# Vision-transformer tower: the last tile's root, normalizing and transposes moved inside four layernorms, fewer products of zeros, and row scatters placed behind a copy

## The reference, cut to what matters

```
h = patches @ W + positions                                  # 592 x 256
h = h + attention(_layernorm(h))                             # 16 heads, rotary parts      (layernorm 0)
h = h + moe_8_experts_top_2(_layernorm(h))                   # shared expert + 8 routed    (layernorm 1)
h = h + selective_scan(_layernorm(h))                        # 16 states, 37 steps         (layernorm 2)
h = h + moe_64_experts_top_8(_layernorm(h))                  # shared expert + 64 routed   (layernorm 3)

def _layernorm(x, axis=-1, eps=1e-05):
    m = jnp.mean(x, axis=axis, keepdims=True)
    v = jnp.var(x, axis=axis, keepdims=True)
    return (x - m) / jnp.sqrt(v + eps)
```

## Time and profile before

| | us |
|---|---|
| median of three executions | 437.95 |
| the profiled execution, its own time | 443.19 |
| its span from first to last instruction | 441.5 |
| PE busy | 415.7 |
| DVE busy | 255.6 |
| ACT busy | 139.9 |
| POOL busy | 156.1 |

### The profile page before, as it was taken

The page is one execution under the profiler, slowest core; times in us unless marked ns, Lnnn a source line. Parts: engine busy times, 40 slices in busy tenths (PEclk is TensorE's granted clock), DMA queues, the critical chain, the costliest instruction groups (busy, mean ns, idle before and its releaser), DMA issues. The chain is left out here.

```text
span 441.5 us, 8821 instructions
## 1 busy us (share of the span) xinstructions
PE 415.7 (94%) x2977; PEld 333.0 (75%) x2985; DVE 255.6 (58%) x643; ACT 139.9 (32%) x352; POOL 156.1 (35%) x129
## 2 busy tenths in 40 slices
PE   8999999888997999999999899998998999999993
PEld 5665567766786999999976389886776788888872
DVE  0548878765850111221353789998775656655545
ACT  1040068783321111112204865552401223232210
POOL 2007834540056100010470168761001156545560
PEclk9999999999898999999999989999899999999998
DMA  8863096001067768874250233321025477787453
GB/s 265 234 174 114 2 293 234 3 1 57 1 254 263 254 211 255 282 265 141 88 163 35 80 110 109 106 62 43 15 72 152 150 180 198 174 201 176 109 128 105
DMA packets 32078, 63.57 MB, mean 144 GB/s; under 512 B 6063, under 2 KB 19678, under 8 KB 29742
## 3 DMA queue, kind: packets, MB, share of 16 engines
q1 hardware_dynamic: 26381, 50.90, 36.9%
q0 software_dynamic: 5664, 12.25, 10.9%
HBM read 50.51 MB, written 12.63 MB: 143 GB/s over the span
## 5 line engine op out<-in xcount | busy, mean ns | idle before, releaser
L1891 PE MATMUL PS<-xT,w1s 128*128 128x296 f32 x224 | 62.2, 422 | 0.0
L1891 PEld LDWEIGHTS PS<-xT,w1s 128*128 128x128 f32 x224 | 42.4, 195 | 11.7 <-issue 1.1
L1839 PE MATMUL PS<-ident,scratch 128*128 128x128 f32 (+1 forms) x340 | 43.6, 281 | 1.2 <-DVE scratch L1278 1.1
L629 POOL DMA_INDIRECT scratch<-xg,idx_nxt x18 | 17.9, 996 | 73.0 <-DVE idx_nxt L1412 38.6
L1272 DVE TENSOR_TENSOR_SCAN scratch<-scratch,PS 128x592 f32<-128x592 f32 x32 | 41.9, 1366 | 2.9 <-PE PS L1846 2.9
L1839 PEld LDWEIGHTS PS<-ident,scratch 128*128 128x128 f32 (+1 forms) x340 | 38.8, 183 | 5.2 <-DVE scratch L1278 2.2
L1195 DVE COPY scratch<-PS 128x144 f32<-128x144 f32 (+1 forms) x16 | 5.1, 319 | 64.2 <-PE PS L1765 64.2
L1756 PE MATMUL PS<-scratch,w0up 128*128 128x144 f32 (+1 forms) x256 | 37.6, 307 | 3.6 <-DVE scratch L1178 3.3
L1756 PEld LDWEIGHTS PS<-scratch,w0up 128*128 128x128 f32 x256 | 35.9, 196 | 5.6 <-DVE scratch L1178 4.2
L1906 PE MATMUL PS<-w1s,scratch 128*128 128x256 f32 (+1 forms) x140 | 34.7, 381 | 1.3 <-DVE h L1315 1.1
L785 ACT ACTIVATE scratch<-PS 128x288 f32<-128x288 f32 (+1 forms) x32 | 13.8, 430 | 67.8 <-PE PS L1756 59.6
(11 more groups left out here) (332 smaller groups left out, 756.9 us busy)
## 6 DMA issues: line engine op xcount, KB each, us to landing
w0dn<-in_w0dn SPq DMA_DIRECT2D x9, 1024.0 KB, 5.2
w0up<-in_w0up SPq DMA_DIRECT2D x9, 1024.0 KB, 5.9
w0dn<-in_w SPq DMA_DIRECT2D x16, 384.0 KB, 3.9
scratch<-rows_c SPq DMA_DIRECT2D x14, 296.0 KB, 3.3
by_expert<-zeros SPq DMA_DIRECT2D x2, 1920.0 KB, 13.2
w1s<-in_w SPq DMA_DIRECT2D x14, 256.0 KB
w1s<-in_w SPq DMA_DIRECT2D x14, 128.0 KB, 3.5
w0up<-in_patchesT SPq DMA_DIRECT2D x6, 296.0 KB, 4.6
```

The lines of the kernel that those rows point to most:

```text
L629: nc.gpsimd.indirect_dma_start(xe1[:, half, q, :], None, xg, bass.IndirectOffsetOnAxis(ap=idx_nxt[:, q:q + 1], axis=0)).then_inc(xe1_in[q] ...
L1839: last = mm(PS[0:ROWS[t], t // 2, (t % 2) * D + c * P:(t % 2) * D + (c + 1) * P], src[:, t * P:t * P + ROWS[t]], ident[:, :], start=False, ...
L1891: last = mm(PS[:, 2 * n + j, 0:HALF], w1s[:, s, w:w + F1], xT[:, c, half(n)], start=c == 0, stop=c == 1)
```

## The change

There are eight edits.

1. On POOL, the wait for `xeT_ready` moves from between the fourth and fifth scatter to ahead of the first.
2. On ACT, in every layernorm, the root of tile 4 moves ahead of the copy of the transposed tiles (L678).
3. On DVE, in layernorm 1 alone, the inverse and normalizing of tile 4 move ahead of the copy L914.
4. On DVE, in layernorm 2, `add_late(4)` moves from ahead of the inverse L901 to behind the normalizing of tiles 0 and 1.
5. On PE, for layernorms 0 and 3, the transposes of tile 4 move ahead of the products of tile 2.
6. On PE, for layernorm 1, ten products of zeros become five, three become one, and the transposes of tile 4 follow at once with two products of zeros behind them; they stood behind the logits of tiles 0 to 3.
7. On PE, four groups of four products of zeros ahead of layernorm 2's transposes become four groups of one.
8. On PE, behind layernorm 2, the transposes of tile 4 move between the two dt products of the first half, and the first quarter of u is made with the rest of u and no longer ahead of the second half of dt.

```diff
--- before.py
+++ after.py
@@ -556,9 +556,8 @@
                         bass.IndirectOffsetOnAxis(ap=idx0[:, s, j:j + 1], axis=0)).then_inc(xe_in[s], 16)
             for s in range(SLOTS0):
                 pool.wait_ge(y_out[s], 16)
+            pool.wait_ge(xeT_ready, 1)
             for t in range(NTILE):
-                if t == 2:
-                    pool.wait_ge(xeT_ready, 1)
                 for k in range(K0):
                     nc.gpsimd.indirect_dma_start(
                         rows_by_expert, bass.IndirectOffsetOnAxis(ap=slots[0:ROWS[t], k, t:t + 1], axis=0),
@@ -674,11 +673,10 @@
                 for t in (2, 3):
                     nc.scalar.activation(xn[:, t, :], normed_from(l, t), ACT.Identity, bias=xshift[:, t:t + 1],
                                          scale=rstd[:, t:t + 1]).then_inc(xn_act, 1)
+                act.wait_ge(var_ready, 2 * l + 2)
+                nc.scalar.activation(std[:, b:NTILE], mv[:, b:NTILE, 1], ACT.Sqrt, bias=LN_EPS).then_inc(std_ready, 1)
                 act.wait_ge(xT_mm, 2 * l + 1)
                 nc.scalar.copy(xT[:, 1, a * P:b * P], PS[:, XT_BANK[l] + 1, 0:(b - a) * P]).then_inc(xT_hi, 1)
-                a, b = LN_PARTS[1]
-                act.wait_ge(var_ready, 2 * l + 2)
-                nc.scalar.activation(std[:, a:b], mv[:, a:b, 1], ACT.Sqrt, bias=LN_EPS).then_inc(std_ready, 1)
 
             layernorm(0)
             for t in range(NTILE):
@@ -910,11 +908,17 @@
                 last_tile()
                 settle()
                 nc.vector.bn_aggr(mv[:, NTILE - 1, :], stats[:, NTILE - 1, :]).then_inc(var_ready, 1)
+                def normalize_last():
+                    dve.wait_ge(std_ready, 2 * l + 2)
+                    link(nc.vector.reciprocal(rstd[:, b:NTILE], std[:, b:NTILE]))
+                    normalize(NTILE - 1)
+
+                if l == 1:
+                    normalize_last()
                 dve.wait_ge(xT_mm, 2 * l + 1)
                 nc.vector.tensor_copy(xT[:, 0, a * P:b * P], PS[:, XT_BANK[l], 0:(b - a) * P]).then_inc(xT_lo, 1)
-                dve.wait_ge(std_ready, 2 * l + 2)
-                link(nc.vector.reciprocal(rstd[:, b:NTILE], std[:, b:NTILE]))
-                normalize(NTILE - 1)
+                if l != 1:
+                    normalize_last()
                 dve.wait_ge(xT_mm, 2 * l + 2)
                 nc.vector.tensor_copy(xT[:, :, b * P:NPAD],
                                       PS[:, XT_BANK[l] + 2, 0:2 * P].rearrange("p (c n) -> p c n", c=2)).then_inc(xT_lo, 1)
@@ -1227,7 +1231,11 @@
                 if t in LATE:
                     add_late(t)
                 close_tile(t)
-            layernorm(2, lambda: close_tile(NTILE - 1), lambda: add_late(NTILE - 1))
+            def last_rows():
+                add_late(NTILE - 1)
+                close_tile(NTILE - 1)
+
+            layernorm(2, last_rows)
             dve.wait_ge(a_exp, 1)
             nc.vector.tensor_scalar(a_neg[:, :, :], a_neg[:, :, :], -1.0, None, ALU.mult).then_inc(a_ring_ready, 1)
             nc.vector.memset(barA.rearrange("p r (b t) -> p r b t", b=B)[:, :, :, 0:1], 0.0).then_inc(a_ring_ready, 1)
@@ -1512,8 +1520,8 @@
             transpose_xn(0, range(NTILE - 1), 3)
             pe.wait_ge(attn_in, 9 * 16)
             for t in range(NTILE):
-                if t == NTILE - 1:
-                    transpose_xn(0, (t,))
+                if t == 2:
+                    transpose_xn(0, (NTILE - 1,))
                 if t in (0, NTILE - 1):
                     need_xT(0, t // (NTILE - 1))
                 for c in range(2):
@@ -1681,12 +1689,11 @@
             project_out(4)
 
 
-            keep_busy(7, 10)
-            transpose_xn(1, range(NTILE - 1), 3)
+            keep_busy(7, 5)
+            transpose_xn(1, range(NTILE - 1), 1)
+            transpose_xn(1, (NTILE - 1,), 2)
             pe.wait_ge(route_in, 10 * 16)
             for t in range(NTILE):
-                if t == NTILE - 1:
-                    transpose_xn(1, (t,))
                 if t in (0, NTILE - 1):
                     need_xT(1, t // (NTILE - 1))
                 for c in range(2):
@@ -1790,7 +1797,7 @@
                 last.then_inc(late_mm, 1)
             for t in range(1, NTILE):
                 pe.wait_ge(yg_in[0][t], 16)
-                keep_busy(7, 4)
+                keep_busy(7, 1)
             pe.wait_ge(dtw_ready, 3)
             transpose_xn(2, range(NTILE - 1), 3)
             def make_u(c, n):
@@ -1798,19 +1805,20 @@
                     last = mm(PS[:, 2 * c + n, 0:HALF], w_in[:, k, c * P:(c + 1) * P], xT[:, k, half(n)], start=k == 0, stop=k == 1)
                 return last
 
+            need_xT(2, 0)
             for n in range(2):
                 if n:
-                    make_u(0, 0)
-                    transpose_xn(2, (NTILE - 1,))
-                need_xT(2, n)
+                    need_xT(2, 1)
                 for c in range(2):
+                    if c and not n:
+                        transpose_xn(2, (NTILE - 1,))
                     for k in range(2):
                         last = mm(PS[:, 4 + 2 * c + n, 0:HALF], dt_w[:, k, c * P:(c + 1) * P], xT[:, k, half(n)],
                                   start=k == 0, stop=k == 1)
                     if n:
                         last.then_inc(dt_mm, 1)
             for c in range(2):
-                for n in range(c == 0, 2):
+                for n in range(2):
                     last = make_u(c, n)
                 last.then_inc(u_mm, 1)
             pe.wait_ge(sp_taken_max, 1)
@@ -1876,8 +1884,8 @@
             transpose_xn(3, range(NTILE - 1), 3)
             for p, (a, b) in enumerate(ROUTER_PARTS):
                 for t in range(a, b):
-                    if t == NTILE - 1:
-                        transpose_xn(3, (t,))
+                    if t == 2:
+                        transpose_xn(3, (NTILE - 1,))
                     if t in (0, NTILE - 1):
                         need_xT(3, t // (NTILE - 1))
                     for c in range(2):
```

## The result

| | before | after |
|---|---|---|
| median of 20 executions each, us | 438.88 (436.70 to 441.13) | 437.06 (434.98 to 439.65) |
| the profiled execution, us | 443.19 | 437.35 |
| its span, us | 441.5 | 435.7 |

The ratio is 0.9954, with a 95% interval of 0.9935 to 0.9972. The kernel became 1.8 us faster. The forecast was 430.0 us with a range up to 434.5 us. So the sign was right, and some 7 us of the gain are missing. The profiled execution of before lies above all twenty of its kernel, and the last part comes back to that.

The account below looks back on a forecast made before the run. PE, or the DVE chain it waits for, was taken to bound all four layernorms. Terms 0.66 + 1.42 + 1.41 + 0 + 4.0 + 0.45 = 7.94 us took the 437.95 us median to 430.0 us, range 426.0 to 434.5 us.

Parts of the forecast that it names:

- The step that failed: Scatters at the first routed item: later scatters stay covered, gain 0; up to 5.0 us cost if cover were gone.
- what would make the prediction wrong: Further 8s on the clock line, or a wait for a DMA or POOL ahead of the item's products L1756.
- the third rival: First item's gather cancels 3.5 us of layernorms 0 and 1: 433.5 us, 438.5 with scatters uncovered; chance 0.09.
- start to the statistics of layernorm 1: Layernorm 0: tile 4's products start at 25.95 instead of 26.61 us, a gain of 0.66 us.
- Layernorm 1: Layernorm 1 and router: 1.42 us from the new order, 1.41 us more if the clock stays up, otherwise 0.
- Layernorm 2: Layernorm 2 up to the scan: fewer products of zeros and reordered dt and u gain 4.0 us, bounds 3.1 and 4.15.
- Layernorm 3: Layernorm 3 up to the router's choice: 0.45 us gained, bounds 0.15 and 0.66, since DVE's chain limits PE.
- The scan's start: Start of the scan: 1.5 us more gain where PE's broadcasts of the third state run at full clock.
- The copy is freed: First item's copy no longer held: 2.16 us and up to 1.7 us of clock, 426.1 to 427.9 us; chance 0.25.
- The clock takes part back: Fewer products of zeros let the clock fall behind the router and in further places: 431.4 to 434.8 us; chance 0.23.
- Slower: Behind layernorm 2, PE starts cold and stays at the lower clock level: 442.6 us; chance 0.06.

Follow-up runs that it names:

- e1: Changed kernel with the scatter edit alone undone (four scatters ahead of the wait for the copy, six behind): 431.24 us, ratio 0.9814.
- e2: Kernel before with the scatter edit alone (all ten scatters behind the copy): 443.51 us, ratio 1.0090.
- e8: e1 with the removed products of zeros of layernorms 1 and 2 put back, the two behind tile 4's transposes kept: 435.10 us, ratio 0.9914.
- e16: e1 without the products of zeros of layernorm 2, those of layernorm 1 left: 431.03 us, ratio 0.9824.
- e6: Kernel before with the layernorm 1 edits alone, including the earlier root of tile 4 on ACT: 437.12 us, ratio 0.9976.
- e4: Kernel before with the layernorm 2 edits alone, including the earlier root of tile 4 on ACT: 435.31 us, ratio 0.9920.
- e3: Changed kernel with POOL's wait for the copy taken out altogether: 431.72 us, ratio 0.9824.
- e11: e1 with a wait on SP that holds the refill of w0dn until all scatters have landed: 432.78 us, ratio 0.9856.
- e13: Changed kernel with half of each refill of w0dn left out, so it does not compute the reference: 435.58 us, ratio 0.9919.
- e7: Kernel before with the early transposes of layernorms 0 and 3 and the earlier root of tile 4 on ACT: 437.93 us, ratio 0.9983.
- e10: e2 with a wait on SP that holds the refill of w0dn until all scatters have landed: 444.64 us, ratio 1.0135.
- e12: e1 with no products of zeros in layernorms 1 and 2: 434.03 us, ratio 0.9899.
- e18: e1 with sixteen products of zeros on PE ahead of every second wait for an item's rows: 444.14 us, ratio 1.0138.
- e9: Changed kernel with a wait on SP that holds the refill of w0dn until all ten scatters have landed: 436.05 us, ratio 0.9934.
- e5: Changed kernel with two scatters ahead of the wait for the copy and eight behind it: 431.52 us, ratio 0.9849.
- e17: Changed kernel with sixteen products of zeros on PE ahead of every second wait for an item's rows: 444.06 us, ratio 1.0121.

## Why the prediction was wrong

**The step that failed** is that of the scatters. It had the load of the next item move "to about 153 us", needed "at 160.50 us", and went on: "That is 7.5 us for a transfer, so this delay lies under the products of items 0 and 1." It was priced at 0 with 5.0 us as what it costs uncovered. It cost 5.8 us (e1 beside the result; 6.1 by the ratios) and 4.9 us (e2). Three things were off in it.

- *The need.* Start of the load and need were read off a profile whose items ran slow. The earlier trace rows has 160.50 - 133.28 = 27.22 us between transposes that stand 23.42 us apart in e1: it holds the late copy and the slow clock of slice 13. So 3.8 us of the cover were of that execution. e1 shows 3.7 us to spare; the step reckoned with 7.5 us for a transfer of some 5.
- *The delay.* It was 7.2 us relative to PE, not 5.0. Four scatters ahead of the copy had POOL's time from before the transposes; behind it all ten start 2.0 us after them. And the landing is 1.4 us later still, behind a weight refill. The step moved the load by the time of issue alone. The [3.87 <-issue] ahead of L575 in the earlier trace rows is that landing; it is 6.37 us in e1 and 7.79 us in the changed kernel. In the execution of the earlier trace rows the slow first item had put the refill off until 144.81 us, behind the last scatter, so that the landing looked short as well:

```profile
144.81 0.34 SPq L454 DMA_DIRECT2D w0up<-in_w0up  x1
```

- *What else hangs on the landing.* PE's idle wait brought a fall of the clock, worth 1.3 us in the profile and up to some 2.2 us by the medians (5.8 less 3.65). The prediction had clock terms elsewhere but none for this wait.

That a wait for a DMA stands ahead of the item's products was named as what would make the prediction wrong, and as the half of the third rival with "the delay of the scatters no longer covered". It had a chance of 0.09, and 437.06 lies inside its 433.5 to 438.5 us. Its other half, a gather that holds back what the layernorms gained, did not occur: the first item's transposes came 17.36 us behind L1727, where it had been 17.40. (It does occur in the profiles of e8 and e16, with 18.5 us.)

**The other steps**, in the two profiled executions, from stage to stage:

| stage | forecast gain, us | before | after | gain | in other traces |
|---|---|---|---|---|---|
| start to the statistics of layernorm 1 | 0.66 | 102.21 | 101.36 | 0.85 | 100.6 to 101.7 with edits 2 and 5, 101.71 with edit 2 alone (e6), 102.22 in e2 |
| to the first products behind the choice (L1720, L1727) | 1.42 + 1.41 | 13.67 | 10.85 | 2.82 | e2, without the edits and without a fall: 12.29 |
| to the first item's transposes | 0 | 17.40 | 17.36 | 0.0 | 17.3 to 17.8; e8 and e16 18.5 |
| to L1788 (L1795) | 0 | 82.83 | 84.23 | -1.4 | e1 79.09, e2 83.92 |
| to the last step before the scan (L1260, L1268) | 4.0 | 33.79 | 29.42 | 4.4 | e2 33.79, e1 29.42 |
| to the transposes of layernorm 3 | 0 | 56.85 | 58.48 | -1.6 | e1 56.24, e2 58.49 |
| to L1924 (L1932) | 0.45 | 14.48 | 13.71 | 0.8 | e2 13.81, e4 and e6 13.72 |
| to the end | 0 | 120.27 | 120.29 | 0.0 | |

- *Layernorm 1.* Without a fall of the clock the new order takes 10.85 us and the old one 12.29: 1.44 us, as forecast (1.42). The other 1.4 us are the fall. The forecast put it into the sum, with 0 as the other bound. But it comes and goes: with the change's order and its products of zeros, four of the twelve profiled executions still show it (e1, e3, e11, e13) and eight don't; with the old order four of five do (before, e4, e7, e10) and e2 doesn't. So the edits may make it rarer, and these few traces don't show that.
- *Layernorm 2.* 4.4 us, where 4.0 were forecast; the stage takes 33.8 us in the five profiles with the old order there (before, e2, e6, e7, e10), and 29.3 to 29.9 us in the twelve with the change's order and products of zeros. The start of the dt products gives 2.6 of it (forecast 2.56).
- *Layernorm 3.* The gain of 0.8 us is the fall of slice 29, which before had and e2 had not. The edits are worth 13.81 - 13.71 = 0.1 us, below the forecast's own bound of 0.15, and e4 and e6, which keep PE's old order there, have 13.72: edit 5 bought nothing in layernorm 3.

All terms together were forecast at 7.94 us, and e1 measured 7.35, with 6.5 to 9.8 us as its interval. So the sum without the scatters stands within what can be measured.

**The scan's start.** The forecast allowed 1.5 us more where the third state's broadcasts run at full clock. The changed kernel's profile went the other way: 6.8 us at the lower level, and it lost 1.6 us there against before. The length of the scan falls into three classes over all profiles: 56.2 to 56.4 us with no fall at its start (e1, e4, e8, e12, e16, e18), 56.8 with a short one (before and eight others), 58.5 with a long one (the changed kernel, e2, e7, e10, e11). Of the last, e2, e7 and e10 leave layernorm 2's products as they were before. So the fall needs no edit 7. What sets it off stays open.

**The rivals.** *The copy is freed* (0.25): nothing was to be freed; the hold was in one execution. *The clock takes part back* (0.23): right that a fall would cost the forecast, wrong about the main place, since the one that edit 1 paid for came from the wait. *Slower* (0.06): PE did not stay cold behind layernorm 2; its stage took 29.42 us as in e1.

The difference between the profiled execution of before and the median, taken as the same in both, wasn't: before's own profile lies 4.3 us above its median, the changed kernel's 0.3. By the table the former holds a fall behind the router (1.4 us), a slow first item (3.7 us over e1's stage) and short falls in the scan and in slice 29 (0.6 and 0.7 us).

## What to carry to other kernels

When a wait is moved ahead of a row of DMA issues, reckon the slack of everything behind them relative to the engine that will need it, and in an execution that has no stalls of its own in that stretch; a stall lends cover that other executions do not have. Then add to the delay of issue what the transfers in flight at that moment add to the landing, and to the wait the clock that falls in it. Products of zeros can be trimmed as long as the stretch behind them keeps its clock: here most of them cost their full length, and the last eight ahead of the router paid for themselves.

## What the runs showed of the hardware

- A landing depends on what else is in flight. The load of 192 KB took 4.7 us in e1 and 7.3 us in e9, where two weight refills of 1 MB each were issued in the 2.4 us ahead of it. From the end of the last scatter's issue to the start of the load behind it, POOL stands for 6.2 to 7.8 us in the fourteen profiles in which SP issued a weight refill 1.7 to 2.5 us ahead of that end. It stands for 3.9 to 4.7 us in the six in which the refills nearest to it were issued over 4 us ahead, at most 0.2 us ahead, or behind it (before, e5, e8, e9, e10, e16). The Trainium skill (DMA: Bandwidth & Descriptors, "Queues, rings and completion order") says that each transfer engine takes turns between its queues; that transfers of different queues slow each other in these rows agrees.
- An idle wait of PE of 3.65 us brought 3.4 us at the lower level right behind it, and 1.3 us more until the next item; with products of zeros in the wait the fall was gone (e17). A shorter wait brings it in some executions only: e9's 2.47 us was followed by a fall (10.66 us to the next item), e10's 2.56 and e13's 2.25 us were not (9.14 us each).
